# One accumulator in place of two: routed and shared rows added straight into the output of an AdaLN block

## The chip, the cores and the metric

One NeuronCore of a Trainium2 chip runs the whole block. The metric is the device time of one execution in microseconds (us); a kernel is judged by the median of several timed runs. One more execution was profiled, and all rows below come from its trace.

## The reference

Two batches of 1024 tokens with 256 channels go through linear attention and a mixture of experts. `mod` gives each batch six rows of 256; `ga` and `gb` are the gate rows of the two halves.

```python
mod = (silu(c) @ wmod).reshape(B, 6, 1, -1)
sa, ca, ga, sb, cb, gb = (mod[:, i] for i in range(6))
ga, gb = (sign(g) * maximum(abs(g), 0.25) for g in (ga, gb))
h = layernorm(x) * (1 + ca) + sa
x = x + ga * linear_attention(h)          # this x is called x1 below
h = layernorm(x) * (1 + cb) + sb
scores = sigmoid(h @ w_router)            # 32 experts, 6 chosen of 4 groups out of 8
routed = sum(score[t, e] * (silu(h @ gate_w[e]) * (h @ up_w[e])) @ down_w[e]
             for the 6 experts e chosen for token t)
shared = silu(h @ sh_gate_w) * (h @ sh_up_w) @ sh_down_w
out = x + gb * (routed + shared)
```

## The kernel before

**Up to the routing.** Tokens stand in 16 tiles of 128 rows, 8 to a batch, in groups of four. PE, ACT and DVE do the first norm, the attention and the projection; DVE adds the projection to x, which gives x1 in `X`, and takes its statistics. POOL turns the variances into deviations (`second_deviation`, lines 511 and 512). DVE makes the second norm (`second_norm`, lines 943 and 948), PE the router's logits and DVE the choice of six experts per token. For each group of tiles DVE writes row numbers into `rows_i`, and POOL stores each token's normed row, with a record (the scores of its 32 experts and its number), into `pair_rows` in memory, once per chosen expert: 96 indirect stores of 128 rows (`dispatch`, line 560). Rows of one expert stand together there, so that an expert's pairs can be cut into blocks of 128.

**The map.** DVE and PE work out which expert owns which block and where its rows begin, and put it on one partition as whole numbers (`map_i`). There are up to 128 blocks in turns of four (`R`); the number of turns is read from the map. `blocks` runs a step per turn on every engine: the first turn is written out, then loops follow, and the last turn is written out again. In the written-out turns the block's number n is a plain number, in the loops it is a register.

**A block.** SP loads 128 rows and 128 records. PE turns the rows (line 1439), DVE copies them (line 1112), PE multiplies by gate and up weights (line 1446), ACT and DVE make silu(gate) * up, PE turns that (line 1454), ACT copies it, PE multiplies by the down weights (line 1461). ACT weighs the result by the pair's score (line 778) into one of four slots `yw`. DVE picks the score (line 1122) and the token's number (`dest`, line 1129). POOL adds the 128 rows to their tokens by an indirect accumulating transfer, a *scatter* (line 588). Even blocks go to `token_sums0` and odd ones to `token_sums1`, two accumulators in memory.

**Order of additions.** An accumulating transfer reads its destination and writes it later, so two that hold the same token must not be under way together. Blocks of one expert hold different tokens, blocks of different experts may share some. So each scatter waits until the scatter two blocks back, which goes to the same accumulator, has landed.

**The other terms.** x1 is divided by the gate row (`divide`, line 903, with the reciprocal of line 889) and stored into `token_sums1` (line 433). The shared expert's rows are stored by ACT into `token_sums0`. **Last stage:** when all scatters have landed, SP fetches `token_sums0`, POOL adds `token_sums1` to it by four accumulating transfers (line 608), DVE multiplies by the gate row (line 1158), and SP stores the output.

## Time and profile before

| | |
|---|---|
| median of three runs | 536.52 us (536.23 to 536.63) |
| the profiled execution | 533.56 us, span of its instructions 531.8 us |
| granted TensorE clock, mean of the span | 0.938 of full speed |
| busy PE / POOL / DVE / ACT | 457.2 / 287.7 / 224.8 / 176.1 us |
| memory traffic | 43.13 MB read, 40.90 MB written |

The span runs from the first instruction to the last; the execution's time has some more around it. Busy time is summed over the span, which has three stretches: the first 230 us (attention, routing, dispatch), the loop over blocks, and the last stage. A rate for one stretch has to be read from that stretch alone.

### The profile page before, as it was taken

Reading aid. Unit: us, or ns where it says so; the run is one execution under the profiler, and the core shown is the slowest. Engines: PE = TensorE matmul, PEld = TensorE weight load, DVE = VectorE, ACT = ScalarE, POOL = GpSimd, SP = SyncE. Lnnn points to the kernel's source line nnn. Section 1 sums busy time; section 2 is a strip of 40 time slices with the busy share of each in tenths; the row PEclk is TensorE's granted clock in tenths of the full one; section 3 lists DMA queues with packets and bytes.
Section 4 is the critical chain, followed back from the end, with each engine's and each line's share of the span. In section 5 each row is a group of like instructions: output and inputs, shape, how many; then the busy total and the mean of one; then the engine's idle time right before and its main releaser. Section 6 shows DMA issues by size and latency. Waiting matters only on the chain.

```text
span 531.8 us, 9471 instructions
## 1 busy us (share of the span) xinstructions
PE 457.2 (86%) x1994; PEld 318.3 (60%) x1995; DVE 224.8 (42%) x971; ACT 176.1 (33%) x429; POOL 287.7 (54%) x257
## 2 busy tenths in 40 slices
PE   4899879798799999349999999999999999999600
PEld 4355656447447655327777777777777777776400
DVE  1934687727875551013333333333333333333202
ACT  2232231222231322104444444444444444444300
POOL 1500711576877777704565556566666556656530
PEclk9999897899898999859999999999999999999955
DMA  8999411133458899535677575666656567666388
GB/s 279 339 334 366 180 41 40 63 129 118 166 146 284 284 302 357 202 89 97 99 117 110 95 119 89 108 114 113 103 98 117 96 104 115 114 97 104 41 247 246
DMA packets 86193, 83.25 MB, mean 157 GB/s; under 512 B 22329, under 2 KB 80155, under 8 KB 86172
## 3 DMA queue, kind: packets, MB, share of 16 engines
q1 hardware_dynamic: 63708, 50.49, 33.3%
q0 software_dynamic: 20160, 30.43, 30.1%
q10 hardware_dynamic: 2304, 2.10, 1.2%
q8 instruction: 8, 0.13, 0.1%
q14 instruction: 13, 0.11, 0.1%
HBM read 43.13 MB, written 40.90 MB: 158 GB/s over the span
## 4 chain that ended last, share of the span: by engine, by line
PE 79%; DMA 7%; DVE 5%; issue 3%; ACT 2%; POOL 2%; SPq 1%; POOLq 0%; ACTq 0%
PE bank L1446 23%; PE bank L1461 17%; PE bank L1363 8%; PE bank L1263 6%; PE bank L1439 5%; PE bank L1454 4%; PE bank L1374 4%; PE bank L1249 3%; DMA gate_up<-token_sums 2%; PE bank L1165 2%; PE bank L1336 2%; DMA token_sums<-tok_buf,dest 2%; DMA XH<-in_L_attn_x 1%; PE bank L1197 1%; PE bank L1301 1%
## 5 line engine op out<-in xcount | busy, mean ns | idle before, releaser
L588 POOL DMA_INDIRECT token_sums<-tok_buf,dest x104 | 161.4, 1552 | 118.7 <-ACT tok_buf L778 51.4
L1446 PE MATMUL bank<-gate_up,tok_buf 128*128 x416 | 141.3, 462 | 0.4 <-DVE tok_buf L1112 0.4
L1112 DVE COPY tok_buf<-bank 128x256 f32<-128x256 f32 x104 | 44.1, 424 | 187.3 <-PE bank L1439 185.4
L560 POOL DMA_INDIRECT pair_rows<-XH,rows_i x96 | 94.9, 989 | 44.3 <-issue 28.4
L1461 PE MATMUL bank<-down,tok_buf 88*128 x416 | 109.0, 384 | 0.0
L1446 PEld LDWEIGHTS bank<-gate_up,tok_buf 128*128 128x128 f32 x416 | 79.4, 191 | 29.1 <-issue 1.7
L1461 PEld LDWEIGHTS bank<-down,tok_buf 88*128 88x128 f32 x416 | 70.6, 190 | 7.6 <-issue 0.2
L778 ACT ACTIVATE tok_buf<-bank,tok_buf 128x256 f32<-128x256 f32 x104 | 49.2, 473 | 53.2 <-PE bank L1461 52.6
L763 ACT ACTIVATE tok_buf<-bank 128x176 f32<-128x176 f32 x104 | 33.0, 317 | 91.2 <-PE bank L1446 91.2
L1439 PEld LDWEIGHTS bank<-ident,tok_buf 128*128 128x128 f32 x208 | 27.4, 142 | 48.5 <-issue 24.0
L1439 PE MATMUL bank<-ident,tok_buf 128*128 128x128 f32 x208 | 41.2, 280 | 17.6 <-DMA tok_buf<-pair_rows 14.6
L769 ACT ACTIVATE tok_buf<-bank 88x256 f32<-88x256 f32 x104 | 39.4, 379 | 17.6 <-PE bank L1454 6.9
L1363 PE MATMUL bank<-tok_buf,sh_gu 128*128 128x512 f32 (+1 forms) x96 | 44.6, 623 | 0.0
L1454 PE MATMUL bank<-ident,tok_buf 128*88 128x128 f32 x208 | 39.7, 273 | 0.0
L1118 DVE TENSOR_TENSOR tok_buf<-tok_buf,bank 128x176 f32<-128x176 f32 x104 | 34.0, 327 | 4.0 <-ACT tok_buf L763 4.0
L1263 PE MATMUL bank<-down 128*128 128x512 f32 x64 | 33.1, 654 | 0.0
L1363 PEld LDWEIGHTS bank<-tok_buf,sh_gu 128*128 128x128 f32 (+1 forms) x96 | 18.3, 192 | 23.6 <-issue 23.5
L547 POOL TENSOR_TENSOR XH<-XH,down 128x256 f32<-128x256 f32 x16 | 11.0, 718 | 28.6 <-DVE down L872 28.6
L1122 DVE SCALAR_TENSOR_TENSOR tok_buf<-iota_e,own_expert,tok_buf 128x32 f32<-128x32 f32 x104 | 25.6, 246 | 0.1
L1454 PEld LDWEIGHTS bank<-ident,tok_buf 128*88 128x88 f32 x208 | 23.9, 122 | 0.5 <-issue 0.2
L1374 PE MATMUL bank<-sh_dn,sT 128*128 128x256 f32 (+1 forms) x96 | 23.4, 402 | 0.0
L1374 PEld LDWEIGHTS bank<-sh_dn,sT 128*128 128x128 f32 (+1 forms) x96 | 19.2, 202 | 3.8 <-issue 0.5
(153 smaller groups left out, 433.5 us busy)
## 6 DMA issues: line engine op xcount, KB each, us to landing
tok_buf<-pair_rows SPq DMA_DIRECT2D x104, 128.0 KB
gate_up<-in_L_ffn_gate_w SPq DMA_DIRECT2D x8, 704.0 KB, 8.2
gate_up<-in_L_ffn_up_w SPq DMA_DIRECT2D x8, 704.0 KB, 9.0
down<-in_L_ffn_down_w SPq DMA_DIRECT2D x2, 2816.0 KB
pair_rows<-sh_rows SPq DMA_DIRECT2D x1, 5120.0 KB, 18.9
XH<-in_L_attn_x SPq DMA_DIRECT2D x4, 512.0 KB, 10.1
token_sums<-sh_rows ACTq DMA_DIRECT2D x16, 128.0 KB, 6.2
gate_up<-token_sums SPq DMA_DIRECT2D x4, 512.0 KB, 5.4
```

What stands on the lines that cost most here:

```text
L560: nc.gpsimd.indirect_dma_start(out=pair_rows, out_offset=bass.IndirectOffsetOnAxis(ap=rows_i[:, t, k:k + 1], axis=0), in_=XH[:, t, :], in_ ...
L588: nc.gpsimd.indirect_dma_start(out=token_sums[c % 2], out_offset=bass.IndirectOffsetOnAxis(ap=dest[:, c:c + 1], axis=0), in_=yw[:, c, :], ...
L769: nc.scalar.activation(aT[0:KD, c % 2, :, :], banks[3][0:KD, 0:2 * P].rearrange("p (m n) -> p m n", m=2), ACT.Copy).then_inc(aT_copied, 1)
L778: nc.scalar.activation(yw[:, c, :], banks[4 + c % 2][:, 0:C], ACT.Copy, scale=pair_weight[:, c:c + 1]).then_inc(y_scaled, 1)
L1112: V.tensor_copy(xT[:, c % 2], banks[0][:, 0:C].rearrange("p (k n) -> p k n", k=KC)).then_inc(xT_copied, 1)
L1263: last = mm(ps[:, :], hT[:, k, a:a + P], wT[:, k, C:3 * C], start=k == 0, stop=k == KC - 1)
L1363: last = mm(ps[0:n, :], sh_gu[:, s, k, a:a + n], h2T[:, b, k, g * W:(g + 1) * W], start=k == 0, stop=k == KC - 1)
L1374: last = mm(ps[:, 0:C], sT[0:n, m, i * P:(i + 1) * P], sh_dn[0:n, m, :], start=m == 0, stop=m == len(SC) - 1)
L1439: last = nc.tensor.transpose(banks[0][:, k * P:(k + 1) * P], xg[:, s, k * P:(k + 1) * P], ident[:, :])
L1446: last = mm(banks[1 + c % 2][:, 0:M2], xT[:, c % 2, k, :], gate_up[:, bass.ds(e * (KC * M2) + k * M2, M2)], start=k == 0, stop=k == KC - 1)
L1454: last = nc.tensor.transpose(banks[3][0:KD, m * P:(m + 1) * P], act[:, c % 2, m * KD:(m + 1) * KD], ident[:, :])
L1461: last = mm(banks[4 + c % 2][:, 0:C], aT[0:KD, c % 2, m, :], down[0:KD, bass.ds(e * C + m * E * C, C)], start=m == 0, stop=m == 1)
```

## The change

The two accumulators, the division by the gate row and the last stage are gone; the output itself is the accumulator.

- SP stores x1 to the output as each group of four tiles is done, and the second norm, which overwrites x1, waits for that store.
- POOL multiplies the shared expert's down weights by the gate rows before its first dispatch. The weights of batch 1 go to memory and back into the place of those of batch 0 when these have been used.
- ACT copies the shared rows into free places of `XH` (`homes`), and POOL adds them to the output by four accumulating transfers: the first after 60 dispatches, three behind the last dispatch. POOL waits for all four before its first scatter.
- A record gets two more numbers, 1 and 0 for a token of batch 0, 0 and 1 for one of batch 1. In each block ACT and DVE make the row's gate from them (`gate_of_first`, `make_gate`), and DVE, no longer ACT, weighs the result by score and gate (`weigh`). It waits for the landing of the scatter four blocks back, which read the same slot.
- The map has a third section: 16 for a block that is the first of its expert, else 0. POOL reads it by four register loads a turn (line 618 of the changed kernel). A scatter waits for the landings of the three blocks before it where that number is 16, and else for none that is less than four blocks back.
- On POOL `blocks` writes out two turns in place of one. In these, n is a plain number, and the wait counts don't hold `fresh`.

```diff
-    REC = E + 1
+    REC = E + 1 + B
...
-        gb_dram = nc.dram_tensor("gate_rows", (1, B * C), f32).ap()
-        token_sums = [nc.dram_tensor(f"token_sums{a}", (T, C), f32).ap() for a in range(2)]
-        sums_v = [a.rearrange("(b p i) c -> p b i c", b=B, p=P) for a in token_sums]
+        gated_down = nc.dram_tensor("gated_shared_down", (SM, C), f32).ap()
+        tokens_out = out.rearrange("b n c -> (b n) c")
...
+        homes = [XH_flat[:, a * HOME:a * HOME + GT * C].rearrange("p (i c) -> p i c", c=C) for a in range(NT // GT - 1)]
+        row_gate = [XH_flat[:, a * HOME + GT * C:(a + 1) * HOME] for a in range(2)]
...
-        def blocks(eng, step):
+        def blocks(eng, step, apart=1):
             last_turn = load_last_turn(eng)
-            step(0, False)
-            with eng.Fori(1, FEWEST) as turn:
+            for turn in range(apart):
+                step(turn, False)
+            with eng.Fori(apart, FEWEST) as turn:
...
-            sp.wait_ge(gb_ready, B)
-            sp.dma_start(gb_dram, gate_rows[0:1, :]).then_inc(gb_stored, 16)
             for b in range(B):
                 for g in range(NG):
                     n = b * NG + g
-                    sp.wait_ge(divided, n + 1)
-                    rows_g = sums_v[1][:, b, g * GT:(g + 1) * GT, :].rearrange("p (k i) c -> p k (i c)", k=KC)
-                    sp.dma_start(rows_g, shares[b][g]).then_inc(shares_stored[n], 16)
+                    await_read(sp, ("proj", b, (g + 1) * GT - 2))
+                    await_read(sp, ("proj", b, (g + 1) * GT - 1))
+                    sp.dma_start(out_v[:, b, g * GT:(g + 1) * GT, :], X[:, n * GT:(n + 1) * GT, :]).then_inc(x1_stored[n], 16)
+                if b == 0:
+                    sp.wait_ge(down_gated, 1)
+                    for m, (a, n) in enumerate(SC):
+                        sp.dma_start(gated_down[a:a + n, :], second_down[0:n, m, :]).then_inc(gated_stored, 16)
...
+                sp.dma_start(sh_dn[0:n, m, :], gated_down[a:a + n, :]).then_inc(gated_back, 16)
...
-            for s in range(0, R, 2):
+            for g in range(NT // GT):
+                sp.wait_ge(x1_stored[g], 16)
+                sp.wait_ge(shared_added[g], 16)
+            for s in range(R):
                 sp.wait_ge(scattered[s], 16 * last_turn + 16)
-            for g in range(NT // OT):
-                t = g * OT
-                sp.dma_start(sums[:, 0, t:t + OT, :], sums_v[0][:, t // TB, t % TB:t % TB + OT, :]).then_inc(fetched[g], 16)
-            sp.dma_start(gb_again.rearrange("p b c -> p (b c)"), gb_dram.partition_broadcast(P)).then_inc(gb_back, 16)
-            for s in range(1, R, 2):
-                sp.wait_ge(scattered[s], 16 * last_turn + 16)
-            sp.sem_inc(all_scattered, 1)
-            for g in range(NT // OT):
-                t = g * OT
-                sp.wait_ge(out_ready, g + 1)
-                sp.dma_start(out_v[:, t // TB, t % TB:t % TB + OT, :], sums[:, 0, t:t + OT, :]).then_inc(stored, 16)
-            sp.wait_ge(stored, 16 * NT // OT)
+            sp.sem_inc(finished, 1)
...
+            def gate_shared_down():
+                pool.wait_ge(heads_clear, 16)
+                pool.wait_ge(gb_ready, B)
+                pool.wait_ge(ld_sh, 16 * (2 + len(SC)))
+                link(nc.gpsimd.tensor_copy(gates[:, :, :], gb))
+                for m, (a, n) in enumerate(SC):
+                    last = nc.gpsimd.tensor_tensor(second_down[0:n, m, :], sh_dn[0:n, m, :], gates[0:n, 1, :], ALU.mult)
+                link(last)
+                for m, (a, n) in enumerate(SC):
+                    last = nc.gpsimd.tensor_tensor(sh_dn[0:n, m, :], sh_dn[0:n, m, :], gates[0:n, 0, :], ALU.mult)
+                last.then_inc(down_gated, 1)
+            def add_shared(g, home):
+                pool.wait_ge(shared_ready, (g + 1) * GT)
+                pool.wait_ge(x1_stored[g], 16)
+                nc.gpsimd.dma_start(out_v[:, g // NG, g % NG * GT:(g % NG + 1) * GT, :], homes[home],
+                                    accum_op=ALU.add).then_inc(shared_added[g], 16)
             second_deviation(0, 0)
             second_deviation(0, 1)
-            pool.wait_ge(heads_clear, 16)
+            gate_shared_down()
             dispatch(0, 25)
             second_deviation(1, 0)
             dispatch(25, 32)
             second_deviation(1, 1)
-            dispatch(32, NT * TOPK)
+            dispatch(32, 60)
+            add_shared(0, 0)
+            dispatch(60, NT * TOPK)
+            for g in range(1, NT // GT):
+                add_shared(g, g % (NT // GT - 1))
             for g in range(NT // GT):
-                pool.wait_ge(shares_stored[g], 16)
-            for s in range(2):
-                pool.wait_ge(sh_stored[s], 16 * (NT // 2))
-            def scatter(c, n, turns):
+                pool.wait_ge(shared_added[g], 16)
+            def scatter(c, n, base, fresh):
+                for j in range(1, min(n, R - 1) + 1 if isinstance(n, int) else R):
+                    count = base if c >= j else base - 16
+                    pool.wait_ge(scattered[(c - j) % R], count if isinstance(count, int) else count - 16 + fresh)
                 pool.wait_ge(y_scaled, n + 1)
                 pool.wait_ge(dest_ready, n + 1)
-                wait(pool, scattered[(c - 2) % R], 16 * turns)
                 pool.sem_inc(pool_passed, 1)
                 nc.gpsimd.indirect_dma_start(
-                    out=token_sums[c % 2], out_offset=bass.IndirectOffsetOnAxis(ap=dest[:, c:c + 1], axis=0),
+                    out=tokens_out, out_offset=bass.IndirectOffsetOnAxis(ap=dest[:, c:c + 1], axis=0),
                     in_=yw[:, c, :], in_offset=None, bounds_check=T - 1, oob_is_err=False,
                     compute_op=ALU.add).then_inc(scattered[c], 16)
             def step(turn, last):
+                fresh = [pool.value_load(map_i[0:1, bass.ds(2 * MAP_W + R * turn + c, 1)], min_val=0, max_val=16)
+                         for c in range(R + last)]
                 for c in range(R):
                     n = R * turn + c
-                    if not first(n):
-                        scatter((c - 1) % R, n - 1, turn + (c == R - 1))
+                    if c > 0:
+                        scatter(c - 1, n - 1, 16 * turn + 16, fresh[c])
+                    elif not first(n):
+                        scatter(R - 1, n - 1, 16 * turn, fresh[c])
                     if last and c == R - 1:
-                        scatter(c, n, turn + 1)
-            blocks(pool, step)
-            pool.wait_ge(all_scattered, 1)
-            for g in range(NT // OT):
-                t = g * OT
-                pool.wait_ge(fetched[g], 16)
-                nc.gpsimd.dma_start(sums[:, 0, t:t + OT, :], sums_v[1][:, t // TB, t % TB:t % TB + OT, :],
-                                    accum_op=ALU.add).then_inc(summed[g], 16)
+                        scatter(c, n, 16 * turn + 16, fresh[c + 1])
+            blocks(pool, step, 2)
...
+            def gate_of_first(c, turn, n):
+                act_e.wait_ge(rec_loaded[c], 16 * turn + 16)
+                if not isinstance(n, int) or n >= 2:
+                    act_e.wait_ge(y_scaled, n - 1)
+                nc.scalar.activation(row_gate[c % 2], gates[:, 0, :], ACT.Copy,
+                                     scale=rec[:, c, E + 1:E + 2]).then_inc(first_gate, 1)
...
-                        link(V.reciprocal(gate_rows, gate_rows))
+                dve.wait_ge(x1_stored[b * NG + g], 16)
...
+            V.tensor_scalar(mapf[:, 33:34], block[:, 0:1], 0.0, 16.0, ALU.is_le, ALU.mult)
...
+            def make_gate(c, n):
+                dve.wait_ge(first_gate, n + 1)
+                V.scalar_tensor_tensor(out=row_gate[c % 2], in0=gates[:, 1, :], scalar=rec[:, c, E + 2:E + 3], in1=row_gate[c % 2],
+                                       op0=ALU.mult, op1=ALU.add).then_inc(gate_made, 1)
+            def weigh(c, turn, n):
+                dve.wait_ge(y_done, n + 1)
+                dve.wait_ge(weight_ready, n + 1)
+                dve.wait_ge(gate_made, n + 1)
+                if not first(turn):
+                    dve.wait_ge(scattered[c], 16 * turn)
+                V.scalar_tensor_tensor(out=yw[:, c, :], in0=banks[4 + c % 2][:, 0:C], scalar=pair_weight[:, c:c + 1],
+                                       in1=row_gate[c % 2], op0=ALU.mult, op1=ALU.mult).then_inc(y_scaled, 1)
...
+                        make_gate((c - 1) % R, n - 1)
+                        weigh((c - 1) % R, turn if c > 0 else turn - 1, n - 1)
...
+                    pe.wait_ge(gated_back if b else down_gated, 16 * len(SC) if b else 1)
```

POOL ahead of the loop and in the first two turns, before: the last dispatches, one register load (line 364, the number of turns), and scatters that alternate between the accumulators.

```order
L560 DMA pair_rows<-XH,rows_i 67584x320 [waits rows_ready] x64
L364 TENSOR_LOAD down [waits x1_shares_stored3,shared_rows_stored0,x1_shares_stored2,shared_rows_stored1,x1_shares_stored1,x1_shares_stored0]
L364 ISA x2
L588 DMA token_sums0<-tok_buf,dest 2048x256 [waits y_scaled,destinations_ready]
L588 DMA token_sums1<-tok_buf,dest 2048x256 [waits y_scaled,destinations_ready]
L588 DMA token_sums0<-tok_buf,dest 2048x256 [waits scattered0,y_scaled,destinations_ready]
```

The same place after. Line 579 is an addition of shared rows, line 361 the load of the number of turns, 618 the loads of the map's third section, 611 a scatter; `scattered0` to `scattered3` count the landings of each slot.

```order
L558 DMA pair_rows<-XH,rows_i 67584x320 [waits rows_ready] x36
L579 DMA out_0<-XH 128x1024 [waits x1_stored1,shared_rows_ready]
L579 DMA out_0<-XH 128x1024 [waits x1_stored2,shared_rows_ready]
L579 DMA out_0<-XH 128x1024 [waits x1_stored3,shared_rows_ready]
L361 TENSOR_LOAD down [waits shared_rows_added2,shared_rows_added3,shared_rows_added1,shared_rows_added0]
L361 ISA x2
L618 TENSOR_LOAD down
...
L611 DMA out_0<-tok_buf,dest 2048x256 [waits y_scaled,destinations_ready]
L611 DMA out_0<-tok_buf,dest 2048x256 [waits destinations_ready,scattered0,y_scaled]
L611 DMA out_0<-tok_buf,dest 2048x256 [waits destinations_ready,y_scaled,scattered1,scattered0]
...
L611 DMA out_0<-tok_buf,dest 2048x256 [waits y_scaled,destinations_ready,scattered0,scattered2,scattered1]
L611 DMA out_0<-tok_buf,dest 2048x256 [waits y_scaled,destinations_ready,scattered1,scattered3,scattered2]
```

The additions and five loads now stand between the last dispatch and the first scatter, and scatters two and three of the list wait for the landing of every scatter ahead of them; those of the second written-out turn name three.

One turn of POOL's loop, before:

```order
L356 REGISTER_ALU [waits destinations_ready,y_scaled]
L588 DMA token_sums1<-tok_buf,dest 2048x256 [waits scattered1]
L584 REGISTER_ALU
L588 DMA token_sums0<-tok_buf,dest 2048x256 [waits scattered2,y_scaled,destinations_ready]
L584 REGISTER_ALU
L588 DMA token_sums1<-tok_buf,dest 2048x256 [waits scattered3,y_scaled,destinations_ready]
L584 REGISTER_ALU
L356 ISA [waits destinations_ready,y_scaled]
L588 DMA token_sums0<-tok_buf,dest 2048x256 [waits scattered0]
```

And after, from the third of the turn's four loads to its second scatter:

```order
L618 TENSOR_LOAD down
L618 ISA x3
L618 TENSOR_LOAD down
L618 ISA x2
L607 ISA
L611 DMA out_0<-tok_buf,dest 2048x256 [waits y_scaled,destinations_ready,scattered0,scattered2,scattered1]
L607 REGISTER_ALU
L608 REGISTER_ALU [waits scattered1,scattered2,scattered3]
L611 DMA out_0<-tok_buf,dest 2048x256 [waits y_scaled,destinations_ready]
L607 REGISTER_ALU
L607 REGISTER_ALU [waits scattered0]
```

Four loads stand ahead of the turn's first scatter, which is that of the turn before's last block. Later scatters wait for three semaphores, with the register that holds the count worked out in between.

One block on DVE, before:

```order
L1112 COPY tok_buf<-bank0 128x256 [waits gate_up_done,x_turned]
L1118 TENSOR_TENSOR tok_buf<-tok_buf,bank1 128x176 [waits act_turned,silu_done]
L1129 SCALAR_TENSOR_TENSOR dest<-own_expert,tok_buf 128x1 [waits pool_passed_waits]
L1122 ISA [waits block_records_loaded3]
L1122 SCALAR_TENSOR_TENSOR tok_buf<-iota_e,own_expert,tok_buf 128x32
```

And after:

```order
L1111 COPY tok_buf<-bank0 128x256 [waits gate_up_done,x_turned]
L1121 SCALAR_TENSOR_TENSOR XH<-gates,tok_buf,XH 128x256 [waits first_batch_gate_made]
L1117 TENSOR_TENSOR tok_buf<-tok_buf,bank1 128x176 [waits act_turned,silu_done]
L1130 SCALAR_TENSOR_TENSOR tok_buf<-bank4,tok_buf,XH 128x256 [waits row_gate_made,scattered2,pair_weight_ready,y_done]
L1140 SCALAR_TENSOR_TENSOR dest<-own_expert,tok_buf 128x1
L1135 ISA [waits block_records_loaded3]
L1135 SCALAR_TENSOR_TENSOR tok_buf<-iota_e,own_expert,tok_buf 128x32
```

Two operations of 128x256 have joined the block's four: the gate (line 1121) behind the copy of the next rows, and the weighing (line 1130), which waits for PE's result (`y_done`) and for a landing (`scattered2`). The copy of the rows after that (line 1111) is queued behind it.

## Rows read from the trace of the kernel before

**Rows 1.** The page's first part: busy us, share of the span, instructions.

```profile
PE 457.2 (86%) x1994; PEld 318.3 (60%) x1995; DVE 224.8 (42%) x971; ACT 176.1 (33%) x429; POOL 287.7 (54%) x257
```

**Rows 2.** The critical chain, block loop: start us, us, what.

```profile
299.69 1.19 PE bank L1446 x4
...
309.76 1.19 PE bank L1446 x4
```

**Rows 3.** PE's longest waits: us in total, times, longest us.

```profile
PE bank L1439 <- DMA tok_buf<-pair_rows: 14.6, 1, 14.6
```

**Rows 4.** Timeline of POOL, 78 to 147 us: around the first dispatches.

```profile
97.81 1.31 POOL L560 DMA_INDIRECT pair_rows<-XH,rows_i  x1 [15.52 <-DVE rows_i L1031]
...
131.98 1.10 POOL L511 TENSOR_SCALAR rstd<-gate_up 128x4 f32<-128x4 f32 x1 [1.66 <-DVE gate_up L935]
```

**Rows 5.** The critical chain where the block loop begins.

```profile
225.78 2.48 DMA pair_rows<-XH,rows_i
...
230.40 2.17 DMA tok_buf<-pair_rows
```

**Rows 6.** The critical chain from 494 us to the end, same columns.

```profile
498.38 3.79 DMA token_sums<-tok_buf,dest
...
503.00 1.40 POOL token_sums L588
...
505.28 5.96 DMA token_sums<-tok_buf,dest
...
514.12 12.98 DMA gate_up<-token_sums
```

**Rows 7.** Timeline of POOL, two scatters back to back.

```profile
287.22 1.55 POOL L588 DMA_INDIRECT token_sums<-tok_buf,dest  x1 [2.27 <-DVE dest L1129]
289.07 1.55 POOL L588 DMA_INDIRECT token_sums<-tok_buf,dest  x1 [0.30 <-issue]
```

**Rows 8.** All 104 scatters of line L588: us from issue to landing.

```profile
DMA to landing us min/median/max: 2.7/3.9/6.0
```

**Rows 9.** Timeline of PE beside the reciprocal of line 889.

```profile
67.26 0.44 PE L1165 MATMUL bank<-ident,down 128*128 128x128 f32 x2 [1.18 <-DVE down L931]
```

**Rows 10.** The accumulating transfers of the last stage, line L608.

```profile
L608 POOL DMA_DIRECT2D gate_up<-token_sums x4: 949/1172/1477, 511.5 to 514.1; - x4
...
DMA to landing us min/median/max: 5.5/9.4/13.0
```

**Rows 11.** POOL's gatings of x at line L547: busy us, mean ns of one.

```profile
L547 POOL TENSOR_TENSOR XH<-XH,down 128x256 f32<-128x256 f32 x16 | 11.0, 718 | 28.6 <-DVE down L872 28.6
```

**Rows 12.** The four stores of line L433, 512 KB each: us to landing.

```profile
DMA to landing us min/median/max: 2.6/2.7/3.8
```

**Rows 13.** POOL's one register load before the loop, line L364.

```profile
L364 POOLq TENSOR_LOAD <-down x1: 506/506/506, 220.5 to 220.5; - x1
L364 POOLq FUSED_REGOPS  x1: 190/190/190, 221.0 to 221.0; - x1
L364 POOLq SEQ_ASSERT  x1: 32/32/32, 221.2 to 221.2; - x1
```

**Rows 14.** Timeline of POOL at the first scatter.

```profile
243.09 1.62 POOL L588 DMA_INDIRECT token_sums<-tok_buf,dest  x1 [16.35 <-ACT tok_buf L778]
```

**Rows 15.** Timeline of one block: start, us, engine, operation, idle before and releaser.

```profile
303.61 0.42 DVE L1112 COPY tok_buf<-bank 128x256 f32<-128x256 f32 x1 [1.58 <-PE bank L1439]
...
303.95 0.33 DVE L1118 TENSOR_TENSOR tok_buf<-tok_buf,bank 128x176 f32<-128x176 f32 x1
304.20 0.15 DVE L1129 SCALAR_TENSOR_TENSOR dest<-own_expert,tok_buf 128x1 int32<-128x1 int32 x1
```

**Rows 16.** DVE's line L1122, two inputs in SBUF, once per block.

```profile
L1122 DVE SCALAR_TENSOR_TENSOR tok_buf<-iota_e,own_expert,tok_buf x104: 239/245/298, 238.9 to 499.3; 128x32 f32<-128x32 f32 x104
```

**Rows 17.** DVE's groups of 49 to 80 us.

```profile
L943 DVE SCALAR_TENSOR_TENSOR XH<-XH,gate_up,down 128x256 f32<-128x256 f32 x4 | 1.7, 478 | 0.0
...
L868 DVE TENSOR_TENSOR down<-bank,down 128x256 f32<-128x256 f32 x4 | 1.4, 418 | 0.2 <-DVE down L860 0.2
```

115 lines of the change are left out of this document (45 added, 70 removed).

## The prediction

> **What bounds the kernel now.** I read the page's busy line first, then the chain that ended last, then the two transfers at the chain's ends. PE works for 86% of the span, POOL for 54%, DVE for 42% [rows 1]. In the block loop the chain is PE's and repeats every four blocks, 309.76 - 299.69 = 10.07 us, so one block takes 2.52 us [rows 2]. Two stretches are not PE's. Before the loop PE stands for 14.6 us until the first block's rows come [rows 3]; that time belongs to POOL's dispatches, which run from 97.81 [rows 4]; the last starts at 225.78, and the rows are in at 230.40 + 2.17 = 232.57 [rows 5]. After the loop the last scatter lands at 505.28 + 5.96 = 511.24; the sums are then fetched, added and multiplied, of which one transfer alone holds 12.98 us [rows 6], and the span ends at 531.8. The scatters are off the chain except for the last three: POOL can start one every 289.07 - 287.22 = 1.85 us [rows 7], and a landing takes 3.9 us in the median [rows 8]. That is hidden at present because a scatter waits only for the one two blocks back.
>
> **The change, part by part.**
>
> *The last stage goes.* From 511.24 to 531.8 is 20.6 us, all of it fetches, additions and stores that no longer exist, but for the time from the last landing to the program's end. That I set at the 0.83 us that a release by a landing takes (503.00 - 502.17 [rows 6]): **-19.8**, bounds -20.6 and -18.8.
>
> *Ahead of the loop.* The reciprocal goes; it held PE for 1.18 us [rows 9]: -1.2. The first shared-row addition is issued between dispatches 60 and 61 and costs POOL one issue, 0.95 to 1.48 us [rows 10]: +1.3. POOL gates the shared weights with one copy and six multiplications before the first dispatch; 16 products of this kind took 11.0 us [rows 11], so about 5.5 us for the seven. POOL stands idle for 15.52 us there [rows 4], which hides it; uncovered it would cost the whole 5.5. The second norm now waits for a store of 512 KB, 2.7 us [rows 12], where DVE used to divide; DVE is not on the chain there, since POOL waits for nothing but 1.66 us in the whole run of dispatches [rows 4]. PE's later half of the shared rows waits for weights that come back from memory; PE's wait covers a delay of up to 14.6 us [rows 3]. Sum: **0**, bounds -1.2 and +5.
>
> *Start of the scatters.* The three last additions are issued behind the last dispatch (225.78 + 0.96 on the engine, then 3 x 1.17) and land 5.5 to 13.0 us later [rows 10]; with 9.4 that is 239.6. POOL then loads five numbers. The one such load that the trace has took 0.51 + 0.19 + 0.03 us, 0.73 in all, on POOL's sequencer [rows 13]; with the address arithmetic that the order shows ahead of each I take 0.85, so 3.4 us for four, 4.25 for five. The first scatter then starts at about 244.5, against 243.09 [rows 14]. POOL is 1.4 us late when the loop begins; nobody waits for it yet.
>
> *How late POOL may be.* DVE's weighing of block n now needs the landing of block n-4, whose slot it writes. A scatter that starts on time starts about 1 us after its weighing (a release took 0.83 us; I take 1.0), and lands 3.9 later; then DVE needs about 0.55 us to weigh (costed under DVE, below). So POOL may lag by 4 x 2.52 - 1.0 - 3.9 - 0.55 = 4.6 us. Beyond that DVE stands, and with it its copies of the next blocks, and PE: each further us is lost for good. POOL works off a lag at 2.52 - 1.85 = 0.67 us a block, less the loads.
>
> *Loads in the loop.* Four a turn stand ahead of one scatter, and the sequencer cannot pass them. That scatter starts about 4.2 us after its predecessor in place of 2.52: a lag of 1.7 us, worked off in the three blocks behind it. Alone they cost nothing; on top of another lag they count. Bounds: 0 a turn (if they ran wholly beside waits) and 4.0.
>
> *Waits for landings.* A scatter that must wait for the one before it starts 3.9 + 1.1 = 5.0 us after it (0.83 is the row; I take 1.1 because several semaphores are waited for in turn). Which ones wait I worked out from the given inputs: the reference's routing uses 15 of the 32 experts, in 102 blocks, and blocks 14, 28, 29, 30, 32, 33, 46, 52, 59, 60, 68, 69, 85, 101 and 102 are the first of an expert; also blocks 1 to 6, since the code of the first two turns waits for all earlier landings whatever the map says.
> - Blocks 1 to 6: lag 1.4 + 6 x (5.0 - 2.52) = 16.3, and 1.7 more for the loads ahead of block 7, less the 4.6 allowed, is 13.4: **+13.5** with the slower landings of pairs of blocks.
> - Blocks 28 to 33: the six starts are 5.0, 5.0, 4.1 (block 29 has one pair and lands in about 3.0; the shortest landing is 2.7 [rows 8]), 4.2 (loads), 4.3 and 5.2 apart, 27.8 us against 6 x 2.52 = 15.1. With a lag of 1.5 before, less 4.6, 9.6: **+9.5**.
> - Blocks 68 and 69 behind the loads of block 67: 1.5 + 2.5 + 2.5 - 4.6: **+2**.
> - Blocks 14, 46, 52, 59 and 60, 85: the lag peaks at 3 to 4.4 us: nothing, but block 14 and blocks 59 and 60 by a hair.
> - The end: blocks 101 and 102 wait. From the start of scatter 100 to the last landing it is 511.24 - 498.38 = 12.9 us now [rows 6], and 14.3 then: **+1.4**.
>
> *DVE.* Weighing moves to DVE and a row gate is made there per block. Its four operations of one block take 0.42 + 0.33 + 0.15 [rows 15] and 0.25 [rows 16], 1.15 us; the two new ones are of 128x256 like those of 0.48 and 0.42 [rows 17]. The sum is 2.1 of 2.52 us: covered by 0.4; without that cover each 0.1 us over costs 10 us in the run. ACT gives up a weighing for a gate of the same size. An operation with two inputs in SBUF took 239 to 298 ns at all 104 blocks [rows 16], beside 104 scatters of 1.55 us, so a scatter does not hold DVE up. The Trainium skill ("SBUF — State Buffer", "Who interferes with whom") says that a DVE instruction with two SBUF inputs contends with a GpSimd instruction that reads SBUF, and that the later of the two is blocked wholly. If a scatter counted as such a reader, the gate, which has two such inputs, could stand behind one for 1.55 us, DVE would take 3.6 us a block, and the run over 100 us more; the row says that it doesn't. I take 2.1.
>
> Sum: -19.8 + 0 + 13.5 + 9.5 + 2 + 1.4 = **+6.6**. The profiled execution took 533.56 us with a span of 531.8; the median of the runs is 536.52, 2.96 more. The difference is carried to the median: 536.52 + 6.6 = 543.1.
>
> **Rivals.**
> 1. *The loads are cheap* (the other side). If POOL's sequencer ran them during its waits, or one cost under 0.5 us, the three places of lag shrink: by the same recurrence, 0 us a turn takes 10 us off, 533; the point that decides is about 1.9 us a turn. For it: the one load of the trace ran on the sequencer, not on the engine. Against: the sequencer is one stream, a scatter behind a load comes after it, and that load took 0.73 [rows 13]. A landing of 3.5 in place of 3.9 comes to the same, 535.5. Together 0.19.
> 2. *Landings are longer.* Additions to rows that were just written may take 4.3; each 0.2 us costs about 4 us, so 0.4 gives 551. The median of 3.9 holds with up to two in flight [rows 8], and here waits leave mostly one. 0.16.
> 3. *DVE becomes the pacer*, 0.1 us over PE's 2.52 on about 75 undisturbed blocks: +7.5, 550. 0.05.
> 4. *The gating holds up the dispatches.* POOL's seven operations run beside DVE's choice of experts. If each waited for the other, the first dispatch came up to 5.5 us late; the wait of 1.66 us [rows 4] takes some back: +3.8, 547. In the trace no POOL product runs beside that choice, so no row excludes it. 0.08. The rule of the Trainium skill named above ("SBUF — State Buffer", "Who interferes with whom") would have it so; no run here shows it for these operations.
>
> **How the numbers follow.** The likeliest case, with 0.52, is 543.1; its own range is 537 to 549 (landing by 0.2, loads by 0.4 us a turn). Runs of this kernel differ by up to 0.1%, so about 0.2% can be told from no change, 1.1 us. Faster by more than that is rival 1 (0.19) and a little of the likeliest case's lower end: 0.20. Within 0.2%: 0.07. Slower: 0.73. Leaving out the tails of rivals 1 and 2, the range is 531 to 556.
>
> **What would show it.** The last landing should come at 511.24 + 26.4 = 537.6 us, and the span's end within 1 us of it. PE should lose about 13 us between 250 and 290, about 10 between blocks 32 and 38, and nothing in the last 25 blocks; the waits should be DVE's, for scatter landings. POOL's line of scatters should show starts about 5 us apart at blocks 1 to 6. Register loads should appear four a turn, 0.7 to 0.9 us each. The prediction is wrong if a landing of the serial scatters is below 3.5 us, if the loads run beside the waits everywhere, if DVE's busy time per block passes 2.5 us, or if the first dispatch starts later than 98.

## The result, and the profile after

The changed kernel takes 550.93 us (549.22 to 554.28, four runs) against 536.58 of the kernel before: the ratio is 1.0273, with a 95% interval of 1.0222 to 1.0325. It is slower by 14.3 us. The forecast was slower by 6.6, 543.1, so the direction held and the time lies inside the range of 531 to 556, but the loss is more than twice what was forecast. The profiled execution was the slowest of the four, 554.28 us with a span of 552.5; the same kernel profiled once more (first experiment) took 550.15 with a span of 548.3, and where the two differ both are given.

The page's first part, with busy us, share of the span and instructions per engine, answers to [rows 1]:

```profile
PE 473.1 (86%) x1994; PEld 327.0 (59%) x1995; DVE 306.0 (55%) x1172; ACT 169.6 (31%) x429; POOL 292.8 (53%) x268
```

DVE has 81 us more to do, as its two new operations ask. That it does not set the pace is seen in the chain that ended last, in a stretch without waits (start us, us, what), which answers to [rows 2]:

```profile
475.00 1.19 PE bank L1456 x4
...
477.48 1.19 PE bank L1456 x4
...
479.97 1.19 PE bank L1456 x4
```

One block takes 2.49 us here, and the copies of blocks 72 and 98 start 65.9 us apart in both kernels (415.43 to 481.29 us before, 448.59 to 514.47 after). The loop has not become slower as such; it stands still at a few places, and it begins later. This is the chain where it begins, the same stretch as [rows 5]:

```profile
231.46 6.66 SPq L366
...
238.31 4.18 DMA tok_buf<-pair_rows
...
243.26 0.44 DVE tok_buf L1111
...
254.43 3.91 DMA out<-tok_buf,dest
...
259.23 4.80 DMA out<-tok_buf,dest
...
264.91 3.98 DMA out<-tok_buf,dest
```

SP's one load of the map's register values takes 6.66 us, and the first rows take 4.18 to arrive, against 2.17 before. In the chain of the kernel before, SP's load is

```profile
228.34 1.88 SPq L369
```

The first scatter starts at 254.43 instead of 243.09 [rows 14], not at the 244.5 of the prediction. POOL's timeline (start, us, engine, line, operation, idle time before and its releaser) shows what runs beside them, and then the first scatters:

```profile
229.86 2.78 POOL L579 DMA_DIRECT2D out<-XH  x3
254.43 1.60 POOL L611 DMA_INDIRECT out<-tok_buf,dest  x1 [21.80 <-DVE dest L1140]
259.23 1.56 POOL L611 DMA_INDIRECT out<-tok_buf,dest  x1 [3.20 <-DVE dest L1140]
264.91 1.65 POOL L611 DMA_INDIRECT out<-tok_buf,dest  x1 [4.12 <-DMA out<-tok_buf,dest]
269.78 1.54 POOL L611 DMA_INDIRECT out<-tok_buf,dest  x1 [3.21 <-DVE dest L1140]
```

The three late additions are issued from 229.86 on, just ahead of SP's load, and the last of them lands at 231.0 + 11.2 = 242.2, when the first rows are nearly in:

```profile
L579 POOL DMA_DIRECT2D out<-XH x4: 981/1156/1605, 182.1 to 231.0; - x4
...
DMA to landing us min/median/max: 5.5/8.6/11.2
```

The scatters behind the first are 4.5 to 5.7 us apart, 5.0 in the mean over the six up to 284.43, as forecast. A wait for several semaphores is put down to the last event that the trace shows, here often DVE's; by the landings themselves each of the six starts 0.9 to 1.2 us behind the landing of its predecessor (254.43 + 3.91 = 258.34, and the next starts at 259.23).

The last dispatch, too, starts late, at 228.89 instead of 225.78, though the first starts early, at 96.54 instead of 97.81. In between POOL issues the first addition (1.02 us and a gap of 0.3) and waits longer for DVE's statistics of batch 1, 4.88 us (3.84 in the second profile) instead of 1.66 [rows 4]:

```profile
133.97 0.23 POOL L507 TENSOR_SCALAR rstd<-gate_up 128x4 f32<-128x4 f32 x1 [4.88 <-DVE gate_up L931]
```

The end of the program (line, engine, operation: duration ns min/median/max, first and last start us), after and then before:

```profile
L56 POOLq DRAIN  x1: 9118/9118/9118, 543.1 to 543.1; - x1
L56 SPq DRAIN  x1: 7/7/7, 547.2 to 547.2; - x1
```

```profile
L55 POOLq DRAIN  x1: 17466/17466/17466, 514.1 to 514.1; - x1
...
L55 SPq DRAIN  x1: 7/7/7, 531.2 to 531.2; - x1
```

After, SP has seen the last landing and is done at 547.2, but POOL's drain ends only at 543.1 + 9.1 = 552.3, and the span with it. Before, POOL's drain ended at 514.1 + 17.5 = 531.6, 4.5 us behind the landing of its last addition at 514.12 + 12.98 = 527.10 [rows 6], while DVE multiplied and SP stored the last rows until 531.0. There all of it but half a microsecond was covered.

The table says where the time went. Its numbers are us by which DVE's copy of a block's rows starts later than in the kernel before (243.26 against 233.34 at block 0 is 9.9), taken as differences between blocks; "end" is the last landing less that, "tail" the time from the last landing to the span's end less the 20.6 of before. The sum is the difference of the spans from 531.8. A copy feels a late scatter some ten blocks on: the waits of blocks 1 to 6 show in the copies of blocks 11 to 16, those of blocks 28 to 33 in those of 38 to 43. The kernel before has one profile, at 533.56 us, 3 us under its median, and nothing shows in which columns these 3 us are.

| | start (to block 8) | blocks 9 to 27 | 28 to 50 | 51 to 70 | end | tail | sum |
|---|---|---|---|---|---|---|---|
| forecast | 0 | 13.5 | 9.5 | 2 | 1.4 | -19.8 | 6.6 |
| the change | 11.3 | 11.6 | 8.8 | 1.4 | 2.7 | -15.1 | 20.7 |
| the same again | 8.3 | 10.8 | 8.3 | 1.6 | 2.7 | -15.1 | 16.6 |
| first turns by the map | 9.3 | 0.2 | 7.3 | -0.1 | 3.5 | -15.0 | 5.2 |
| no late additions | 4.3 | 12.6 | 8.8 | 1.6 | 2.6 | -15.2 | 14.7 |
| gating earlier | 6.0 | 11.1 | 8.3 | 0.1 | 3.2 | -15.1 | 13.6 |
| a store at the end | 9.5 | 10.4 | 8.1 | 0.2 | 3.5 | -15.1 | 16.5 |
| four sums, no waits | 9.7 | 0 | -0.7 | 0 | -2.4 | -15.1 | -8.5 |
| loads doubled | 9.0 | 18.8 | 13.3 | 8.9 | 12.3 | -15.1 | 47.2 |
| one load a turn | 9.7 | 11.2 | 5.6 | 0.2 | 3.3 | -15.1 | 14.8 |
| three changes | 0.9 | 0.2 | 7.8 | 0.4 | 2.5 | -15.0 | -3.2 |
| three changes and one load a turn | -0.5 | -0.2 | 5.0 | 0 | 3.2 | -15.0 | -7.5 |

### The profile page after: what moved, and what is told of

Same layout as the page of the kernel before. It is cut to its first block, busy times and chain, and to the rows that moved or that the text cites. A ratio compares the mean times of both kernels' runs of the same rounds, so it can differ in the third digit from the quotient of the medians.

```text
span 552.5 us, 10349 instructions
## 1 busy us (share of the span) xinstructions
PE 473.1 (86%) x1994; PEld 327.0 (59%) x1995; DVE 306.0 (55%) x1172; ACT 169.6 (31%) x429; POOL 292.8 (53%) x268
## 4 chain that ended last, share of the span: by engine, by line
PE 60%; DMA 14%; issue 7%; POOL 6%; DVE 6%; ACT 2%; POOLq 2%; SPq 1%; DVEq 0%; ACTq 0%
PE bank L1456 18%; PE bank L1471 13%; DMA out<-tok_buf,dest 12%; POOL pair_rows L558 6%; PE bank L1271 4%; PE bank L1371 4%; PE bank L1449 4%; PE bank L1464 3%; PE bank L1257 3%; PE bank L1173 2%; PE bank L1344 2%; PE bank L1309 2%; PE bank L1384 2%; PE bank L1290 1%; DMA XH<-in_L_attn_x 1%
## 5 line engine op out<-in xcount | busy, mean ns | idle before, releaser
L611 POOL DMA_INDIRECT out<-tok_buf,dest x104 | 163.0, 1568 | 150.2 <-DVE dest L1140 63.0
L1456 PE MATMUL bank<-gate_up,tok_buf 128*128 x416 | 146.2, 475 | 13.2 <-DVE tok_buf L1111 13.2
L1471 PE MATMUL bank<-down,tok_buf 88*128 x416 | 111.3, 391 | 0.0
L1471 PEld LDWEIGHTS bank<-down,tok_buf 88*128 88x128 f32 x416 | 72.5, 194 | 8.0
L1130 DVE SCALAR_TENSOR_TENSOR tok_buf<-bank,tok_buf,XH 128x256 f32<-128x256 f32 x104 | 50.3, 484 | 40.6 <-DMA out<-tok_buf,dest 31.4
L795 ACT ACTIVATE XH<-gates,tok_buf 128x256 f32<-128x256 f32 x104 | 51.7, 497 | 11.5 <-DVE tok_buf L1130 11.5
L1121 DVE SCALAR_TENSOR_TENSOR XH<-gates,tok_buf,XH 128x256 f32<-128x256 f32 x104 | 49.4, 475 | 0.0
L1384 PE MATMUL bank<-sh_dn,sT 128*128 128x256 f32 (+1 forms) x96 | 27.8, 457 | 4.0 <-DMA sh_dn<-gated_shared_down 4.0
L1384 PEld LDWEIGHTS bank<-sh_dn,sT 128*128 128x128 f32 (+1 forms) x96 | 22.3, 236 | 9.1 <-DMA sh_dn<-gated_shared_down 4.1
L1041 DVE TENSOR_TENSOR sT<-sT,bank 128x512 f32<-128x512 f32 (+1 forms) x12 | 8.1, 685 | 34.4 <-PE bank L1371 34.3
```

Of the source, the lines that this page charges most:

```text
L611: nc.gpsimd.indirect_dma_start(out=tokens_out, out_offset=bass.IndirectOffsetOnAxis(ap=dest[:, c:c + 1], axis=0), in_=yw[:, c, :], in_offs ...
L795: nc.scalar.activation(row_gate[c % 2], gates[:, 0, :], ACT.Copy, scale=rec[:, c, E + 1:E + 2]).then_inc(first_gate, 1)
L1121: V.scalar_tensor_tensor(out=row_gate[c % 2], in0=gates[:, 1, :], scalar=rec[:, c, E + 2:E + 3], in1=row_gate[c % 2], op0=ALU.mult, op1=AL ...
L1130: V.scalar_tensor_tensor(out=yw[:, c, :], in0=banks[4 + c % 2][:, 0:C], scalar=pair_weight[:, c:c + 1], in1=row_gate[c % 2], op0=ALU.mult, ...
L1384: last = mm(ps[:, 0:C], sT[0:n, m, i * P:(i + 1) * P], sh_dn[0:n, m, :], start=m == 0, stop=m == len(SC) - 1)
L1456: last = mm(banks[1 + c % 2][:, 0:M2], xT[:, c % 2, k, :], gate_up[:, bass.ds(e * (KC * M2) + k * M2, M2)], start=k == 0, stop=k == KC - 1)
```

## The experiments

All are edits of the changed kernel. Each was timed beside the kernel before on the same chip, which took 536.17 us beside the first four, 536.79 beside the next four and 535.43 beside the last two; so a difference of about 1 us between runs of different groups is not told apart.

**The change once more.** No edit.

> The changed kernel unaltered, for a second profile and for the spread between executions. The profiled execution of the change lost 9.9 us to the kernel before at the loop's first row, 11 us in blocks 9 to 16, 9.3 us in blocks 38 to 45, 1.6 us at block 68, 2.6 us in the last scatters, and gained 15.1 us behind the last landing. If these places are properties of the kernel, each returns within 1 us; what differs between executions should then lie ahead of the loop. If the profiled execution was an odd one, the places move.

Measured: 550.27 us (549.78 to 551.18), ratio 1.0279 (1.024 to 1.0319). Every place behind the start returned within 1 us. The start differed by 3 us: the last dispatch begins at 226.99 instead of 228.89, and SP's load takes 5.68 instead of 6.66. So the places are properties of the kernel, and the spread between these two profiles lies ahead of the loop. One place is not stable: in other profiles with the same loop (gating earlier, a store at the end) blocks 51 to 70 lose 0.1 and 0.2 us, and the end 3.2 and 3.5.

**The first two turns take their counts from the map.**

```diff
-        shared_ready, shared_added = sem("shared_rows_ready"), [sem(f"shared_rows_added{g}") for g in range(NT // GT)]
+        shared_ready = sem("shared_rows_ready")
...
+        shared_added = scattered
...
-                    pool.wait_ge(scattered[(c - j) % R], count if isinstance(count, int) else count - 16 + fresh)
+                    pool.wait_ge(scattered[(c - j) % R], count + fresh)
...
-                    dve.wait_ge(scattered[c], 16 * turn)
+                    dve.wait_ge(scattered[c], 16 * turn + 16)
...
-                sp.wait_ge(scattered[s], 16 * last_turn + 16)
+                sp.wait_ge(scattered[s], 16 * last_turn + 32)
```

> The first two turns take their wait counts from the map too, as the loop does (the shared rows' additions count as a first landing, so that all counts stay positive); blocks 1 to 6 then wait for no landing but that of their slot. Theory: the serial start is lost once and for all, so the copies of blocks 9 to 16 lose nothing more, the crowd at 28 to 33 still costs 9 us, and the whole is 11 to 12 us faster than the change unaltered, 538 to 540. Rival: the loss there comes from the late and cold start of PE (half clock until about 250 us) and from the loads; then it stays and the time moves by less than 3 us.

Measured: 538.89 us (537.57 to 541.99), ratio 1.0062 (1.004 to 1.0084), 11.4 us less than the change unaltered. PE's windows (us, busy us, granted clock, share of DMA, GB/s), first the change, then this kernel:

```profile
260.00:290.00 30.00, 23.69 (x99) 0.94 0.40 67
```

```profile
260.00:290.00 30.00, 30.00 (x144) 1.00 0.68 111
```

PE is busy throughout where it stood 6 of 30 us, and the scatters start with the products, 2.5 us apart:

```profile
252.46 1.60 POOL L612 DMA_INDIRECT out<-tok_buf,dest  x1 [21.47 <-DVE dest L1141]
255.01 1.56 POOL L612 DMA_INDIRECT out<-tok_buf,dest  x1 [0.96 <-DVE dest L1141]
257.50 1.55 POOL L612 DMA_INDIRECT out<-tok_buf,dest  x1 [0.93 <-DVE dest L1141]
```

PE's start is as late as in the second profile of the change (first copy at 241.37 and 241.41), and from 225 to 250 us, behind PE's wait for the first rows, the mean granted clock is 0.66 here and 0.73 there, between its two levels. So the serial start is the cause of the whole loss at blocks 9 to 16, and the late start of PE at a lower clock of none of it. What it is worth, 11 us, is the forecast's 13.5 without its first lag of 1.4 us and with cheaper loads.

**No late additions.** The output lacks the shared rows of three groups of four.

```diff
...
-            for g in range(1, NT // GT):
-                add_shared(g, g % (NT // GT - 1))
-            for g in range(NT // GT):
-                pool.wait_ge(shared_added[g], 16)
+            pool.wait_ge(shared_ready, NT)
+            for g in range(NT // GT):
+                pool.wait_ge(x1_stored[g], 16)
+            pool.wait_ge(shared_added[0], 16)
```

> Leaves out the three additions of shared rows behind the last dispatch (the output lacks the shared rows of three of the four groups); all waits for those rows stay. Theory: these transfers hold up SP's register load (6.66 us instead of 1.88) and the first row load (4.18 instead of 2.17), so both return to their old values and the loop begins 6.8 us earlier; since POOL's scatters start with it, the time falls by 6 to 8 us against the change unaltered. Rival: SP's register load is slow because of the dispatches or the late weights; then only the row load's 2 us come back.

Measured: 545.77 us (543.56 to 548.3), ratio 1.0178 (1.0134 to 1.0223): 4.5 us less, short of the 6 to 8. The mechanism is as expected; the chain where the loop begins:

```profile
231.39 1.87 SPq L366
...
233.44 2.06 DMA tok_buf<-pair_rows
```

Both are back at their old lengths, with the last dispatch as late as in the change's profile (228.81 and 228.89), so it is the additions that hold them up, and not the dispatches. The three changes together (below) compute the whole output and only put the additions off; there the two take 1.87 and 2.06 us as well. Of the 4 to 7 us that the loop's start gains in the table against the two profiles of the change, 1 to 2 are lost again in blocks 9 to 27, so the whole gain does not reach the end.

**Gating earlier.**

```diff
+            gate_shared_down()
             second_deviation(0, 0)
             second_deviation(0, 1)
-            gate_shared_down()
             dispatch(0, 25)
```

> POOL gates the shared weights ahead of the second norm's deviations (about 63 to 68 us) instead of behind them. Theory: DVE's six operations on pairs of sums, which took 0.60 to 0.76 us beside POOL's products and 0.19 to 0.29 before, return to their old length; the first dispatch comes 2 to 3 us earlier and so does the loop, 2 to 4 us in the time. Rival: they are slow for another reason (the store of x1 beside them), or the dispatches wait for PE anyway: the time stays within 1 us.

Measured: 547.27 us (545.86 to 549.06), ratio 1.0222 (1.0176 to 1.0268), 3.0 us less. DVE's operations on the pairs of sums in the kernel before, in the change, and here:

```profile
83.43 0.29 DVE L963 TENSOR_TENSOR gate_up<-XH,gate_up 128x128 f32<-128x128 f32 x1 [2.35 <-ACT XH L701]
83.76 0.22 DVE L969 TENSOR_TENSOR gate_up<-gate_up 128x64 f32<-128x64 f32 x1
...
84.61 0.19 DVE L974 TENSOR_TENSOR gate_up<-gate_up 128x32 f32<-128x32 f32 x1
```

```profile
80.13 0.60 DVE L960 TENSOR_TENSOR gate_up<-XH,gate_up 128x128 f32<-128x128 f32 x1 [2.36 <-ACT XH L719]
80.77 0.63 DVE L966 TENSOR_TENSOR gate_up<-gate_up 128x64 f32<-128x64 f32 x1
...
83.58 0.64 DVE L971 TENSOR_TENSOR gate_up<-gate_up 128x32 f32<-128x32 f32 x1
```

```profile
80.60 0.29 DVE L960 TENSOR_TENSOR gate_up<-XH,gate_up 128x128 f32<-128x128 f32 x1 [2.23 <-ACT XH L719]
80.93 0.23 DVE L966 TENSOR_TENSOR gate_up<-gate_up 128x64 f32<-128x64 f32 x1
...
81.78 0.19 DVE L971 TENSOR_TENSOR gate_up<-gate_up 128x32 f32<-128x32 f32 x1
```

The six take 84.25 - 80.13 = 4.1 us in the change, beside POOL's products (3.2 in its second profile, where two of the six keep their old length), and 1.4 in the two others. The store of x1 is not the cause: in the change it is issued at 77.2 and lands 2.9 us later, as the first of the six begins. The first dispatch starts at 94.30 here, against 96.54 and 97.26 in the two profiles of the change, and 97.81 before. In the chain that ended last this stretch is DVE's in both profiles of the change, and PE's here, as in the kernel before; first the change, then this kernel:

```profile
80.13 0.61 DVE gate_up L960
```

```profile
80.26 4.89 PE bank L1271 x8
```

POOL's wait for the statistics of batch 1 ends at 131.10 here, against 133.97 and 133.32, and with it the last dispatch comes earlier (224.66).

**A store behind the last landing.**

```diff
...
+            sp.dma_start(extra, gate_up[:, 0:1024]).then_inc(extra_stored, 16)
+            sp.wait_ge(extra_stored, 16)
             sp.sem_inc(finished, 1)
```

> Behind the last landing SP stores one more tile of 512 KB to a spare place in memory and waits for it. In the change's profile 5.2 to 5.4 us pass from the last landing to the span's end, while POOL drains; before, POOL's drain ended 4.5 us after its last transfer had landed, beside the last product and store. Theory: the program's end waits for POOL's drain, and SP's store (about 2.7 us) fits beside it: within 1 us of the change unaltered. Rival: the 5 us are the program's end behind SP; then the store adds 2.7 us or more.

Measured: 549.73 us (548.53 to 550.18), ratio 1.0232 (1.0208 to 1.0255), 0.5 us less than the change unaltered, so no cost. The store takes 2.6 us, and POOL's drain still ends behind it, at 539.0 + 9.1 = 548.1:

```profile
L488 SPq DMA_DIRECT2D extra<-gate_up x1: 335/335/335, 543.0 to 543.0; - x1
...
DMA to landing us min/median/max: 2.6/2.6/2.6
```

```profile
L56 POOLq DRAIN  x1: 9120/9120/9120, 539.0 to 539.0; - x1
L56 SPq DRAIN  x1: 7/7/7, 545.7 to 545.7; - x1
```

So the 5 us behind the last landing are POOL's, and 2.6 us of work on SP fit beside them.

**Four sums, no waits.** Scatters go to four spare sums; these are not added to the output.

```diff
...
-                for j in range(1, min(n, R - 1) + 1 if isinstance(n, int) else R):
-                    count = base if c >= j else base - 16
-                    pool.wait_ge(scattered[(c - j) % R], count if isinstance(count, int) else count - 16 + fresh)
...
-                    out=tokens_out, out_offset=...
+                    out=apart_sums[c], out_offset=...
```

> Each of the four slots scatters into a spare sum of its own, and no scatter waits for a landing (the weighing still waits for its slot); the register loads stay. Left out: the sums aren't added to the output. Theory: all waits for landings go, so PE runs at its old pace of 2.5 us a block and loses nothing behind the start; against the change unaltered 10.3 us at blocks 9 to 16, 8.5 at 38 to 45, 1.5 at 68 and some 2.5 at the end: 22 to 24 us faster, 526 to 529. Rival: the register loads or DVE's two new operations hold the loop up by themselves; then a part of it stays, spread over all turns.

Measured: 524.73 us (523.6 to 526.52), ratio 0.9775 (0.9743 to 0.9807), 25.5 us less than the change. PE's windows over the two stretches that lost most, the second one in the change and then both here:

```profile
340.00:370.00 30.00, 24.68 (x104) 0.92 0.40 71
```

```profile
260.00:290.00 30.00, 30.00 (x145) 1.00 0.70 111
340.00:370.00 30.00, 30.00 (x144) 1.00 0.71 112
```

With the loads, DVE's two operations and all else in place, the loop loses nothing behind its start. So neither DVE nor the loads hold it up by themselves. The edit also changes where the scatters go, but that does not shorten a landing: the median is 4.03 us, against 4.05 in the change, both from the landing counts. So it is the waits that cost. The last scatters, which no longer wait, end 2.4 us sooner than before, and that with the loop's losses makes 25 us.

**Loads doubled.**

```diff
+                for c in range(R + last):
+                    pool.value_load(map_i[0:1, bass.ds(2 * MAP_W + R * turn + c, 1)], min_val=0, max_val=16)
                 fresh = [pool.value_load(...) for c in range(R + last)]
```

> POOL makes each of its register loads of the map's third section twice, eight a turn in place of four, 2.5 us more a turn. Theory (the recurrence of the prediction, with 0.62 us a load and the start as measured): a turn's four scatters then need 5.0 + 4 x 1.85 us or a little less against 10.07, so POOL hardly works off a lag any more; the last landing comes 25 us later, 20 to 30 in the time. Rival: the loads run beside the waits for landings and for products; under 6 us.

Measured: 580.7 us (580.17 to 582.93), ratio 1.0824 (1.0791 to 1.0858), 30.4 us more than the change (29.8 when each is taken against the kernel before beside it): the theory's side, at its upper end. DVE's waits for landings, ahead of the weighing, are in us, times and the longest, first in the change and then here:

```profile
DVE tok_buf L1130 <- DMA out<-tok_buf,dest: 31.4, 17, 3.6
```

```profile
DVE tok_buf L1132 <- DMA out<-tok_buf,dest: 73.2, 46, 4.0
```

In the change the copies of blocks 71 to 100 lose 0.1 us in all, with four loads in each turn, so loads cost nothing there. With eight a turn it never gets level again: from the copy of a block's rows to its scatter there pass at least 11.4 us in blocks 9 to 98, against 9.9 in the change where it is level.

**Three changes together.** The first turns by the map, the earlier gating, and this:

```diff
+            for c in range(R):
+                pool.wait_ge(x_loaded[c], 16)
             for g in range(1, NT // GT):
                 add_shared(g, g % (NT // GT - 1))
```

> Three changes together: the first two turns take their counts from the map, the gating stands ahead of the second norm's deviations, and the three late additions wait until the loop's first four blocks of rows have landed. Theory: 11.4 us by the first and 3.0 by the second, as measured; the third gives PE's start back (5 us) but lets the first scatter start only about 5 us behind the first products, at the edge of the 4.6 us that PE bears; 3 to 5 us of it remain. Together 531 to 534, faster than the kernel before. Rival: the late additions only move the loss, since the scatters begin no sooner: 535 to 537.

Measured: 531.54 us (530.02 to 534.58), ratio 0.9917 (0.9887 to 0.9947): 0.8% faster than the kernel before. PE starts 2.7 us earlier than before at block 0 and loses 3.6 up to block 8, since the first scatter starts only at 248.87; the crowd of first blocks at 28 to 33 still costs 7.8. Not all of the earlier start is explained by the edits: POOL's wait for the statistics of batch 1 is 1.18 us here and 4.60 with the earlier gating alone, and the mean granted clock from 90 to 100 us is 1.00, the upper level throughout, against 0.66 there, though PE was busy throughout the 10 us before in both. Why, no run tells.

**One load a turn**, in the change alone and on top of the three:

```diff
-                fresh = [pool.value_load(map_i[0:1, bass.ds(2 * MAP_W + R * turn + c, 1)], min_val=0, max_val=16)
-                         for c in range(R + last)]
+                _, fresh = nc.values_load_multi_w_load_instructions(
+                    map_i[0:1, bass.ds(2 * MAP_W + R * turn, R + last)], engines=(mybir.EngineType.Pool,),
+                    min_val=0, max_val=16)
```

> POOL reads the four numbers of a turn by one register load instead of four, with the same bounds checks. From the profiles, SP's load of eight numbers takes 1.68 us and each check 0.17 to 0.2, so I estimate 1.6 to 1.7 us a turn in place of 2.5. Theory: by the recurrence a turn's loads count only where POOL is behind already, in the first turns and among the firsts of experts: about 3 us off the change unaltered, 547. Rival: what costs is the scatter's waits, not the loads ahead of them: within 1 us.

Measured: 548.29 us (546.16 to 549.19), ratio 1.0224 (1.0185 to 1.0264), 2.0 us less than the change. The direction is the theory's, but with spreads of 1.4 and 3 us in few runs, of different groups, this one comparison does not settle 2 against 3. The table is clearer: the crowd costs 5.6 us instead of 8.3 to 8.8, and the first turns cost 11.2, as they did. So the theory held for the crowd and not for the first turns.

> The three changes tried together before (counts of the first turns from the map, gating ahead of the deviations, late additions behind the first rows) and the one register load a turn. Theory: the same saving of 2 to 4 us where POOL is behind, in the first turns and the crowd: 528 to 530, against 531.5 with four loads and 536.5 of the kernel before. Rival: the crowd's loss is in the landings alone: 531 to 532.

Measured: 527.82 us (526.29 to 529.32), ratio 0.9855 (0.9827 to 0.9883), 3.7 us less than the three changes alone; taken against the kernel before beside each it is 2.4. Of that, 2.8 us are in the crowd of the table, where POOL is behind. This is the fastest version that computes the whole output, 1.45% below the kernel before.

## Why the prediction was right or wrong

*Blocks 1 to 6, 28 to 33, 68 and 69: right.* Forecast 13.5 + 9.5 + 2 = 25.0 us; measured 11.6 + 8.8 + 1.4 = 21.8, and 20.7 in the second profile. The second place shows in the copies of blocks 38 to 43, not 32 to 38 as forecast, and the third is there in some profiles only. Taking away the waits took away all of it (25.5 us with the end), and taking away those of the first turns took away the first part (11.4 us). The recurrence, with a start every 1.85 us, a landing of 3.9 and 1.1 to the next start, holds.

*The loads in the loop: mechanism right, size too high.* The prediction costed one load at 0.85 us from the single load ahead of the loop. The loop's loads (duration ns min/median/max) are shorter:

```profile
L618 POOLq FUSED_REGOPS  x181: 51/147/165, 243.5 to 529.4; - x181
L618 POOLq TENSOR_LOAD <-down x105: 282/290/713, 243.1 to 529.1; - x105
L618 POOLq SEQ_ASSERT  x105: 18/18/24, 243.7 to 529.6; - x105
```

One load with its checks takes 0.63 us, from the start of one to the start of the next in the chain:

```profile
527.20 0.28 POOLq L618
...
527.83 0.28 POOLq L618
```

Four need about 2.5 us a turn, not 3.4. In the prediction's sum for blocks 1 to 6, 0.8 us for the loads ahead of block 7 instead of 1.7, and no first lag of 1.4, give 14.9 + 0.8 - 4.6 = 11.1 for 13.4; the two profiles have 11.6 and 10.8. So the loop's loss was too high by 3 to 4 us, and that hid a part of the two errors below. Rival 1 was right that a load costs less, though not under 0.5 us; that loads run beside the waits fell when doubling them cost 30 us.

*Ahead of the loop: the step that failed most.* "Sum: 0" was 8.3 to 11.3 us, with up to 3 us of that perhaps due to the fast profile of the kernel before. In the change's profile the first copy is 9.9 us late: 3.1 are in the last dispatch (the gating, next paragraph, and the first addition), 4.8 in SP's register load (6.66 against 1.88 us) and 2.0 in the rows. The prediction followed the three late additions to POOL's first scatter, and did not ask what else was under way in the 12 us in which they move (229.86 to 242.2); SP's load and the first rows stand in that very stretch [rows 5]. Without the additions both returned, and the time fell by 4.5 us. The lag of "1.4 us when the loop begins" was absent, since PE itself came late; the prediction's own terms, 239.6 and 4.25, add up to 243.9 and not to its 244.5.

*The gating: rival 4's cost was real, its path was another.* The prediction hid 5.5 us of POOL's work in POOL's 15.52 us of idle time [rows 4] and held DVE to be off the chain there; it gave 0.08, and 3.8 us, to the case that DVE's work beside it suffers and the first dispatch comes late. The first dispatch came early, 96.54 and 97.26 against 97.81, so the sign "later than 98" did not show. But DVE lost 2.7 us there, the six operations taking 4.1 instead of 1.4 us (3.2 in the second profile), on the chain; PE's work behind it and the statistics of batch 1 came later, and POOL's dispatches waited 4.88 and 3.84 us for them instead of 1.66. The move gave 3.0 us back. The Trainium skill ("SBUF — State Buffer", "Who interferes with whom") states that a DVE instruction with two SBUF inputs contends with a GpSimd instruction that reads SBUF; the trace agrees, with 0.60 to 0.76 us in place of 0.19 to 0.29 in the change's profile. In the loop, where that rule was weighed against [rows 16], the row was right: the gate made from two SBUF inputs takes 475 ns beside the scatters, and the loop keeps its 2.49 us.

*The last stage: the second step that failed.* Forecast -19.8; measured -15.1 in both profiles. The prediction let the program end 0.83 us behind the last landing, the time of a release. It took 5.4 us, because POOL's drain ends 5.2 us behind it. That was in the trace of before, under cover of DVE's product and SP's store: POOL's drain ended 4.5 us behind its last landing there. The prediction did not ask what ends next once that cover is gone, and its sign, the span's end within 1 us of the last landing, failed.

*The end of the loop.* 2.7 us against 1.4. From scatter 100 to the last landing it is 547.05 - 532.67 = 14.4 us, as forecast (14.3); the other 1.1 us came ahead of it. In the change the chain there runs through the last turn's five loads (526.4 to 529.6 us), but with one load in their place 526.78 - 498.38 - 26.7 = 1.7 us stand there, so the loads are not the whole cause; the rest is open.

*DVE as pacer, longer landings:* neither. One block takes 2.49 us, and landings are 4.05 us in the median against 3.97 before, from the landing counts of all 104 scatters in both traces (the view of the line, which has only a part of them, says 4.2 against 3.9).

Against the second profile's span, 16.6 - 6.6 = 10.0 us were missed: 8.3 at the start, 4.7 in the tail and 1.3 at the end, less 4.3 that the loop's terms were too high. That the direction and the range still held is in part luck, since the last hid a part of the first two. The medians differ by 14.1 to 14.3 us rather than 16.6 because the profiled execution of before, at 533.56, lay 3 us under its median.

## What to carry to other kernels

When a stage is taken away, look for what ends next behind it, up to the drain of every engine that issued transfers: work hidden by the stage comes into the open with it. When transfers are added, list what every queue does while they move, not only the queue that waits for them; and when an idle engine gets work, ask what the others do beside it. A wait that costs nothing alone is priced by the lag that the engine has when it comes, so loads and waits have to be followed block by block.

## What the runs showed of the hardware

- SP's register load of eight numbers took 1.67 to 1.94 us in the kernel before, in the loop beside scatters too, and 5.4 to 6.7 us at the loop's begin in the changed kernels in which three accumulating transfers of 512 KB were under way; with these left out or put off it took 1.86 to 1.87 us. Why, no run tells.
- POOL's drain ended 5.2 us behind the last landing of its scatters in the change, and 4.5 us behind the last addition in the kernel before. What it does in that time is open.
- One register load of four numbers takes 0.33 us on POOL, one of a single number 0.29; the checks on each number take 0.17 us, so with four numbers they cost more than the load.
